# Linear attention: the row sums of the queries' exponentials taken by VectorE from a transpose, in place of matmuls with a block matrix

## Chip, cores and metric

The kernel runs on one core of one Trainium2 chip. The metric is the device time of one execution in microseconds (us), of which lower is better. Engines: PE is TensorE, PEld its weight loads, DVE is VectorE, ACT is ScalarE, POOL is GpSimd, SP is SyncE, which issues the DMAs.

## The reference, cut to what matters

The program runs four blocks on x, of shape 8 x 256 x 1024 in float32: a linear attention, a feed-forward with 4-bit weights, an autocorrelation attention and a second feed-forward. Only the first block is touched:

```python
def _L0_xattn_ref(q, k, v):
    B, C, N = q.shape            # 8, 256, 1024
    dh = C // H                  # H = 8, so 32 rows to a head
    qh = q.transpose(0, 2, 1).reshape(B, N, H, dh)
    kh = k.transpose(0, 2, 1).reshape(B, N, H, dh)
    vh = v.transpose(0, 2, 1).reshape(B, N, H, dh)
    qh = jax.nn.softmax(qh, axis=3)
    kh = jax.nn.softmax(kh, axis=1)
    kvs = jnp.einsum('bnhd,bnhe->bhde', kh, vh)
    out = jnp.einsum('bnhd,bhde->bnhe', qh, kvs)
    return out.transpose(0, 2, 3, 1).reshape(B, C, N)
...
x = x + jnp.tanh(g_xattn[0]) * _L0_xattn_ref(_layernorm(x, axis=-1), ctx_4096, ctx_4096)
```

The queries' softmax runs over the 32 rows of a head, for each of the 1024 columns. Its denominators are sums over 32 of the 128 rows of a tile.

## The kernel before

`phase_linear_attention` works on 16 tiles of 128 rows x 1024 columns in float32, one tile to a step i, with buffers of two. Each engine runs its own written-out order; `step(i, h)` is that order for one step, and semaphores join the engines. Three stages overlap: step i works on the attention of tile i, finishes the output of tile i-1, and normalises and transposes tile i-2 for the feed-forward that follows.

For one tile the work passes through the engines like this, with the lines of the profile:

- ACT computes `eq`, the exponential of the normalised queries (L417), and `ek`, that of the keys (L421, with its row sums).
- PE transposes `ek` into `psE` (L479). Then it takes the head sums of `eq` (L485): eight matmuls, in each of which a 128x128 piece of `eq` is multiplied with `blk`, a block-diagonal matrix of ones in blocks of 32. The result in `psB` has a column of `eq` on each partition and holds every sum 32 times.
- DVE takes the reciprocal of every 32nd element of it into `rS`, 128x32 (L553).
- ACT spreads each reciprocal over 32 places into `rSx` (L450), PE transposes that back into `psB` (L503), and ACT copies it to SBUF (L456, which releases `turned_done`).
- POOL multiplies `eq` by it (L399). That releases the output matmuls of PE (L492), which run one step later in program order, and DVE adds their result to `X` (L556).
- PE also multiplies the transposed keys with the context (L498), and DVE normalises and masks the product (L568). DVE computes the mean and variance of tiles ahead and behind (L521, L524); POOL turns them into an inverse root (L390, L392) and DVE into an offset (L529).
- ACT normalises the finished tile for the next phase (L463), PE transposes it (L509), and ACT and DVE store it in two half-precision parts (L426, L543). ACT also starts the next phase's weights (L438).

Two orders matter here. On POOL, the multiplication L399 of tile i stands ahead of the inverse root of tile i+2. On DVE, the offset of tile i+2 (L529) stands at the end of a step, and the next step begins with L543, L550 and L553:

```python
def step(i, h):                                   # POOL
    if exists(i - 1):
        rsqrt(i - 1, 1 - h, mv2, ve2, rstd2, mv2_done, rstd2_done)
    if exists(i):
        pool.wait_ge(turned_done, i + 1)
        pool.tensor_tensor(eq[h][:], rSx[:], eq[h][:], ALU.mult).then_inc(eqn_done, 1)
    if exists(i + 2):
        rsqrt(i + 2, h, mv, ve, rstd, mv_done, rstd_done)
```

ACT waits for `rS_done` ahead of L450, and the exponentials of tile i+1 (L417, L421) stand behind L450 in its order. In the last steps `ffn_scales` adds small instructions to every engine.

Of the kernel before, what the change touches and what calls it, by code (L numbers as in the profile page):

```python
# [24 lines left out]
AX = mybir.AxisListType  # L25

P = 128
B, L, D = 8, 256, 1024
# [10 lines left out]
ROWS0 = L // HEADS0  # L39
# [247 lines left out]
def phase_linear_attention(nc, io, res):  # L287
# [9 lines left out]
    with ExitStack() as ctx:  # L297
# [51 lines left out]
        with nc.Block() as block:  # L349
# [61 lines left out]
            @block.scalar  # L411
            def _(act):
                def exponentials(i, h):
                    act.wait_ge(nmr_done, i + 1)
                    after(act, out_mm, i - 1)
                    settle(act)
                    act.activation(eq[h][:], X[:, i, :], ACT.Exp, scale=rstd[h][:], bias=nmr[h][:]).then_inc(eq_done, 1)  # L417
                    after(act, ekT_mm, i - 1)
                    after(act, rks_done, i - 1)
                    act.wait_ge(ncm_done, i + 1)  # L420
                    act.activation(ek[h][:], c_in[h][:], ACT.Exp, bias=ncm[h][:], accum_out=ksum[h][:]).then_inc(ek_done, 1)  # L421

                def turned_high(i):
                    act.wait_ge(xT_mm, i + 1)
                    settle(act)
                    act.activation(halves_of(i, 0), turned_bank(), ACT.Copy, scale=LN_SCALE).then_inc(hi_done, 1)  # L426

                def first_kinks(i):

                    turn, k = divmod(i - 1, len(kinks))  # L430
                    if 0 <= turn < 2:
                        scale, bias, alpha = kinks[k]
                        act.wait_ge(res["first_in"], 16 * (AHEAD // 2) * (turn + 1))
                        if k:
                            act.wait_ge(res["kink_done"], AHEAD // 2 * (i - 1))
                        for u in range(AHEAD // 2 * turn, AHEAD // 2 * (turn + 1)):
                            block_u = res["first"][:, u, :]
                            act.activation(block_u, block_u if k else block_u.bitcast(I32), ACT.Prelu, bias=bias, scale=scale, alpha=alpha).then_inc(res["kink_done"], 1)  # L438

                def step(i, h):  # L440
                    if exists(i):
                        after(act, kv_mm, i - 1)
                        act.wait_ge(ekT_mm, i + 1)
                        act.activation(ekT[h][:], psE[:], ACT.Copy).then_inc(ekT_done, 1)
                    first_kinks(i)
                    if exists(i):
                        after(act, eqn_done, i)
                        act.wait_ge(rS_done, i + 1)

                        act.activation(rSx[:].rearrange("p (n r) -> p n r", r=ROWS0), rS[h][:].unsqueeze(2).to_broadcast([P, D // ROWS0, ROWS0]),  # L450
                                       ACT.Copy).then_inc(rSx_done, 1)
                    if exists(i + 1):
                        exponentials(i + 1, 1 - h)
                    if exists(i):
                        act.wait_ge(rS_mm, i + 1)
                        act.activation(rSx[:], psB[:], ACT.Copy).then_inc(turned_done, 1)  # L456
                    if i == TILES:
                        turned_high(i - 2)
                    if exists(i - 1):
                        after(act, xT_mm, i - 2)  # L460
                        act.wait_ge(nmr2_done, i)
                        settle(act)
                        act.activation(xn[1 - h][:], X[:, i - 1, :], ACT.Identity, scale=rstd2[1 - h][:], bias=nmr2[1 - h][:]).then_inc(xn_done, 1)  # L463
                    if exists(i - 2) and i != TILES:
                        turned_high(i - 2)

                exponentials(0, 0)
                act.wait_ge(const_in, 64)
                act.activation(tg[:], gates[:], ACT.Tanh).then_inc(tanh_done, 1)
                run(act, step, scales_act)  # L470

            @block.tensor
            def _(pe):
                def step(i, h):
                    if exists(i):
                        after(pe, kvm_done, i)
                        pe.wait_ge(ek_done, i + 1)
                        for k in range(KD):
                            mm = pe.transpose(psE[:, k * P:(k + 1) * P], ek[h][:, k * P:(k + 1) * P], ident[:])  # L479
                        mm.then_inc(ekT_mm, 1)  # L480

                        after(pe, turned_done, i)
                        pe.wait_ge(eq_done, i + 1)
                        for k in range(KD):
                            mm = pe.matmul(psB[:, k * P:(k + 1) * P], eq[h][:, k * P:(k + 1) * P], blk[:], start=True, stop=True)  # L485
                        mm.then_inc(sums_mm, 1)
                    if exists(i - 1):
                        pe.wait_ge(eqn_done, i)
                        pe.wait_ge(kvm_done, i)
                        after(pe, x_done, i - 1)  # L490
                        for n in range(2):
                            mm = pe.matmul(psO[:, n * BANK:(n + 1) * BANK], kvm[1 - h][:], eq[1 - h][:, n * BANK:(n + 1) * BANK], start=True, stop=True)  # L492
                        mm.then_inc(out_mm, 1)
                    if exists(i):
                        pe.wait_ge(ekT_done, i + 1)
                        pe.wait_ge(cT_in[h], (i // 2) * 16 + 16 if isinstance(i, int) else (i - h) * 8 + 16)
                        for k in range(KD):
                            mm = pe.matmul(psE[:, 0:P], ekT[h][:, k * P:(k + 1) * P], cT[h][:, k * P:(k + 1) * P], start=(k == 0), stop=(k == KD - 1))  # L498
                        mm.then_inc(kv_mm, 1)

                        pe.wait_ge(rSx_done, i + 1)
                        for k in range(KD):
                            mm = pe.transpose(psB[:, k * P:(k + 1) * P], rSx[:, k * P:(k + 1) * P], ident[:])  # L503
                        mm.then_inc(rS_mm, 1)
                    if exists(i - 2):
                        pe.wait_ge(xn_done, i - 1)
                        after(pe, lo_done, i - 2)
                        for k in range(KD):
                            mm = pe.transpose(psX[:, k * P:(k + 1) * P], xn[h][:, k * P:(k + 1) * P], ident[:])  # L509
                        mm.then_inc(xT_mm, 1)  # L510

                pe.wait_ge(const_in, 64)
                run(pe, step, scales_pe)

            @block.vector
            def _(dve):
# [28 lines left out]
                def step(i, h):  # L545
                    if exists(i - 3) and i != TILES + 1:
                        turned_low(i - 3)
                    if exists(i):
                        dve.wait_ge(ek_done, i + 1)
                        dve.reciprocal(rks[h][:], ksum[h][:]).then_inc(rks_done, 1)  # L550
                        dve.wait_ge(sums_mm, i + 1)

                        dve.reciprocal(rS[h][:], psB[:, 0:D:ROWS0]).then_inc(rS_done, 1)  # L553
                    if exists(i - 1):
                        dve.wait_ge(out_mm, i)
                        dve.scalar_tensor_tensor(X[:, i - 1, :], psO[:], tg[:, 0:1], X[:, i - 1, :], ALU.mult, ALU.add).then_inc(x_done, 1)  # L556
                        if i == TILES:
                            scales_dve(dve, "top")
                        dve.wait_ge(x_done, i)
                        stats(i - 1, 1 - h, st2, mv2, mv2_done)  # L560
                        if i == TILES:
                            scales_dve(dve, "every")
                            turned_low(i - 2)
                    if exists(i):
                        dve.wait_ge(rks_done, i + 1)
                        dve.wait_ge(kv_mm, i + 1)

                        dve.scalar_tensor_tensor(kvm[h][:], psE[:, 0:P], rks[h][:], blk[:], ALU.mult, ALU.mult).then_inc(kvm_done, 1)  # L568
                    if exists(i - 1):
                        offset(i - 1, 1 - h, mv2, rstd2, nmr2, rstd2_done, nmr2_done)  # L570
                    if exists(i + 2):
                        prepare(i + 2, h)
# [2209 lines left out]
```

## Time and profile before

| what | us |
|---|---|
| median of 3 runs (1981.24 to 1986.48) | 1981.4 |
| the profiled execution | 1980.49 |
| its span, first to last instruction | 1978.7 |
| busy in the span: PE | 1917.6 |
| DVE | 1268.1 |
| ACT | 1248.2 |
| POOL | 821.5 |

The span of the profiled execution covers all but 1.8 us of its own time. "Busy" is the time in which an engine has an instruction in it. Matmuls are pipelined and overlap, so that a busy PE can still be short of work. The linear attention occupies about the first 175 us of the span.

### The profile page before, as it was taken

What the parts mean: (1) busy time and instruction counts of PE and PEld (TensorE: products, weight loads), DVE (VectorE), ACT (ScalarE), POOL (GpSimd) and SP (SyncE); (2) the same over time, 40 slices, a digit from 0 to 9 for tenths busy, and PEclk for the clock granted to TensorE, in tenths of its full rate; (3) what the DMA queues carried; (4) which work ended last, traced back from release to release, by engine and by line L of the source; (5) the groups of instructions that cost most, each with busy time, mean ns of one, the idle gap of its engine ahead of it and who ended that gap; (6) DMA issues with size and microseconds to landing.
All of it is one profiled execution on the core that took longest, in us unless ns stands there. A gap on an engine that the chain in (4) does not pass through costs nothing. (4 is left out here: it accounts for less than half of the span.)

```text
span 1978.7 us, 26460 instructions
## 1 busy us (share of the span) xinstructions
PE 1917.6 (97%) x9188; PEld 965.9 (49%) x9188; DVE 1268.1 (64%) x2184; ACT 1248.2 (63%) x1988; POOL 821.5 (42%) x746
## 2 busy tenths in 40 slices
PE   6996999999999999999999999999998899999998
PEld 5774444444444444444444444444444455555544
DVE  5776666573645747365463745546389988888872
ACT  6886888667876777676777767766534434344431
POOL 2433644532222232232322323222268767767742
PEclk9998999999999999999999999999999999999999
DMA  5641633348667383754737466462551110111001
GB/s 208 215 169 54 249 98 100 99 171 283 197 212 235 114 279 109 242 201 165 266 100 265 150 218 205 155 245 83 205 165 33 33 53 27 44 53 38 27 22 43
DMA packets 89972, 288.33 MB, mean 146 GB/s; under 512 B 11760, under 2 KB 16496, under 8 KB 72944
## 3 DMA queue, kind: packets, MB, share of 16 engines
q1 hardware_dynamic: 89840, 286.64, 43.2%
q8 instruction: 74, 1.21, 0.3%
q14 instruction: 58, 0.48, 0.1%
HBM read 259.33 MB, written 27.26 MB: 145 GB/s over the span
## 5 line engine op out<-in xcount | busy, mean ns | idle before, releaser
L1034 ACT ACTIVATE first<-first 128x512 f32<-128x512 f32 (+1 forms) x1024 | 635.8, 626 | 26.3 <-DVE wt L1443 1.8
L1268 POOL TENSOR_TENSOR gu<-wt,gu 128x512 f16<-128x512 f32 x86 | 102.3, 1190 | 388.4 <-ACT gu L1055 388.4
L1443 DVE SCALAR_TENSOR_TENSOR wt<-first,w_scale,absm 128x512 f32<-128x512 f32 x132 | 102.9, 780 | 236.9 <-ACT first L1034 236.4
L1790 PE MATMUL a_psQ<-z,gu 128*128 128x512 f16 x840 | 187.2, 379 | 0.0
L2393 PE MATMUL a_psL<-z,l_x 128*128 128x512 f16 x768 | 170.7, 379 | 0.9 <-DVE l_x L2495 0.8
L1790 PE MATMUL a_psC<-z,gu 128*128 128x512 f16 x660 | 151.3, 379 | 0.0
L1790 PE MATMUL a_psC<-z 128*128 128x512 f16 x612 | 140.4, 379 | 0.0
L1446 DVE SCALAR_TENSOR_TENSOR wt<-a_psE,lora_gain,wt 128x512 f32<-128x512 f32 x132 | 99.1, 751 | 52.3 <-PE a_psE L1748 26.8
L1790 PEld LDWEIGHTS a_psQ<-z,gu 128*128 128x128 f16 x840 | 82.2, 98 | 99.1
L1268 POOL TENSOR_TENSOR dn_lo<-wt,dn_hi 128x512 f16<-128x512 f32 x42 | 49.0, 1167 | 192.3 <-ACT dn_hi L1055 192.3
L1280 POOL TENSOR_TENSOR hid_lo<-z,hid_hi 128x512 f16<-128x512 f32 x68 | 80.9, 1204 | 109.6 <-ACT hid_hi L1096 109.5
L1055 ACT ACTIVATE gu<-wt 128x512 f16<-128x512 f32 x86 | 53.4, 621 | 103.5 <-DVE wt L1446 79.6
L2393 PEld LDWEIGHTS a_psL<-z,l_x 128*128 128x128 f16 x768 | 75.0, 98 | 88.9 <-issue 1.2
L1505 DVE SCALAR_TENSOR_TENSOR X<-a_psL,ffn_gain,X 128x512 f32<-128x512 f32 x132 | 95.3, 745 | 24.5 <-PE a_psL L1847 24.4
L1268 POOL TENSOR_TENSOR z<-wt,z 128x512 f16<-128x512 f32 x51 | 59.8, 1187 | 103.1 <-ACT z L1055 103.1
L1847 PE MATMUL a_psL<-dn_hi,hid_hi 128*128 128x512 f16 x268 | 101.6, 379 | 0.2 <-DVE X L1505 0.2
L1847 PE MATMUL a_psL<-dn_hi,hid_lo 128*128 128x512 f16 x268 | 101.5, 379 | 0.0
L1505 DVE SCALAR_TENSOR_TENSOR X<-a_psQ,ffn_gain,X 128x512 f32<-128x512 f32 x106 | 77.7, 746 | 36.6 <-PE a_psQ L1847 36.6
L1790 PEld LDWEIGHTS a_psC<-z,gu 128*128 128x128 f16 x660 | 63.8, 98 | 74.2
L1505 DVE SCALAR_TENSOR_TENSOR X<-a_psC,ffn_gain,X 128x512 f32<-128x512 f32 x108 | 78.8, 746 | 32.6 <-PE a_psC L1847 32.6
L1847 PE MATMUL a_psL<-dn_lo,hid_hi 128*128 128x512 f16 x254 | 96.2, 379 | 0.0
L1790 PEld LDWEIGHTS a_psC<-z 128*128 128x128 f16 x612 | 59.4, 98 | 70.5
(418 smaller groups left out, 4167.2 us busy)
## 6 DMA issues: line engine op xcount, KB each, us to landing
z<-x_parts SPq DMA_DIRECT2D x126, 1024.0 KB, 6.0
first<-in_codes SPq DMA_DIRECT2D x132, 256.0 KB, 3.0
absm<-in_absmax SPq DMA_DIRECT2D x264, 128.0 KB, 3.4
X<-in_x SPq DMA_DIRECT2D x16, 512.0 KB, 4.4
c_in<-in_ctx SPq DMA_DIRECT2D x16, 512.0 KB, 5.3
cT<-in_ctxT SPq DMA_DIRECT2D x16, 512.0 KB, 3.5
o_sp<-in_w SPq DMA_DIRECT2D x16, 512.0 KB, 4.8
z<-in_ctx SPq DMA_DIRECT2D x8, 1024.0 KB, 7.3
```

The costliest lines, as they stand in the source:

```text
L1034: act.activation(level[w % 2][:], codes[w % RING] if k == 0 else level[w % 2][:], ACT.Prelu, bias=bias, scale=scale, alpha=alpha).then_inc ...
L1055: act.activation(dest(c, name, 0), wt[slot(name)], ACT.Copy).then_inc(whi_done, 1)
L1268: pool.tensor_tensor(low, source, high, ALU.subtract).then_inc(wlo_done, 1)
L1280: pool.tensor_tensor(low, buf, high, ALU.subtract).then_inc(hidlo_done, 1)
L1443: dve.scalar_tensor_tensor(wt[at], source[:], w_scale[:, m:m + 1], absm[w % RING][:], ALU.mult, ALU.mult).then_inc(scaled, 1)
L1446: dve.scalar_tensor_tensor(wt[at], ps_lora[w % 2], lora_gain[:, m:m + 1], wt[at], ALU.mult, ALU.add).then_inc(wt_done, 1)
L1505: dve.scalar_tensor_tensor(dst, ps_ring[down_bank(j, n)], ffn_gain[:], dst, ALU.mult, ALU.add).then_inc(acc_done, 1)
L1790: mm = pe.matmul(out, w[:, k * P:(k + 1) * P], xx[:, k], start=first and q == 0, stop=q == 3 * KD // 2 - 1, skip_group_check=True)
L1847: mm = pe.matmul(ps_ring[down_bank(j, n)], hh[c][:, i * P:(i + 1) * P], w[c][:, hf * BANK:(hf + 1) * BANK], start=(q == 0), stop=(q == len ...
L2393: mm = pe.matmul(sum_bank(d, half), a[:, ks], w[:, k, half * CB:(half + 1) * CB], start=(q == 0), stop=(q == 3 * KD - 1))
```

## The change

The matmul with `blk` becomes a transpose with the identity, so that `psB` holds the exponentials themselves, with a column of `eq` on each partition. DVE then sums each group of 32 elements itself, and takes the reciprocal in place as a second instruction behind a wait on its own semaphore. ACT's wait counts two increments to a tile.

```diff
@@ ACT
                         after(act, eqn_done, i)
-                        act.wait_ge(rS_done, i + 1)
+                        act.wait_ge(rS_done, 2 * i + 2)
@@ PE
                         for k in range(KD):
-                            mm = pe.matmul(psB[:, k * P:(k + 1) * P], eq[h][:, k * P:(k + 1) * P], blk[:], start=True, stop=True)
+                            mm = pe.transpose(psB[:, k * P:(k + 1) * P], eq[h][:, k * P:(k + 1) * P], ident[:])
                         mm.then_inc(sums_mm, 1)
@@ DVE
                         dve.wait_ge(sums_mm, i + 1)
 
-                        dve.reciprocal(rS[h][:], psB[:, 0:D:ROWS0]).then_inc(rS_done, 1)
+                        dve.reduce_sum(rS[h][:], psB[:].rearrange("p (n r) -> p n r", r=ROWS0), AX.X).then_inc(rS_done, 1)
+                        dve.wait_ge(rS_done, 2 * i + 1)
+                        dve.reciprocal(rS[h][:], rS[h][:]).then_inc(rS_done, 1)
```

The order of DVE's instructions around the edit, in a step of the middle of the phase. `made` is the buffer that holds `rS` and the other small tensors; `z` takes the half-precision parts. Before:

```order
L529 SCALAR_TENSOR_TENSOR made<-made 128x1 [waits rstd_done]
L539 TENSOR_SCALAR made<-made 128x1 [waits cmax_done]
L543 SCALAR_TENSOR_TENSOR z<-psX,z 128x2x512 [waits hi_done]
L550 RECIPROCAL made<-made 128x1 [waits ek_done]
L553 RECIPROCAL made<-psB 128x32 [waits sums_mm]
L556 SCALAR_TENSOR_TENSOR X<-psO,tg,X 128x1024 [waits out_mm]
```

And with the change:

```order
L529 SCALAR_TENSOR_TENSOR made<-made 128x1 [waits rstd_done]
L539 TENSOR_SCALAR made<-made 128x1 [waits cmax_done]
L543 SCALAR_TENSOR_TENSOR z<-psX,z 128x2x512 [waits hi_done]
L550 RECIPROCAL made<-made 128x1 [waits ek_done]
L553 TENSOR_REDUCE made<-psB 128x32 [waits sums_mm]
L555 RECIPROCAL made<-made 128x32 [waits rS_done]
L558 SCALAR_TENSOR_TENSOR X<-psO,tg,X 128x1024 [waits out_mm]
```

One instruction has come in, in the same place of the order; the lines behind it are numbered higher by two. On the other engines no instruction has come, gone or moved.

## Rows read from the trace of the kernel before

**Rows 1.** Busy time of each engine in one step (count of instructions), then granted clock
```profile
105.16:114.48 9.32, 8.54 (x63) 7.06 (x61) 7.23 (x16) 8.26 (x11) 3.91 (x5) 1.00 0.51 171
```

**Rows 2.** Timeline, one step: start us, us, engine, line, idle before
```profile
104.11 1.00 ACT L456 ACTIVATE wt<-psB 128x1024 f32<-128x1024 f32 x1
...
105.19 2.36 POOL L399 TENSOR_TENSOR eq<-wt,eq 128x1024 f32<-128x1024 f32 x1 [0.45 <-ACT wt L456]
105.25 1.97 PE L485 MATMUL psB<-blk,eq 128*128 128x128 f32 x16
...
107.61 1.98 PE L492 MATMUL psO<-eq,made 128*128 128x512 f32 x4 [0.39 <-POOL eq L399]
107.82 0.57 POOL L392 TENSOR_TENSOR made<-made,mhalf 128x1 f32<-128x1 f32 x1
...
108.43 0.16 DVE L529 SCALAR_TENSOR_TENSOR made<-made 128x1 f32<-128x1 f32 x1 [0.81 <-POOL made L392]
...
108.57 1.22 DVE L543 SCALAR_TENSOR_TENSOR z<-psX,z 128x1024 f16<-128x1024 f32 x1
...
109.77 0.34 DVE L553 RECIPROCAL made<-psB 128x32 f32<-128x32 f32 x1
...
110.20 1.06 ACT L450 ACTIVATE wt<-made 128x1024 f32<-128x1024 f32 x1 [1.06 <-DVE made L553]
...
111.31 1.09 PE L503 MATMUL psB<-ident,wt 128*128 128x128 f32 x8
...
112.30 1.13 ACT L421 ACTIVATE ek<-c_in,made 128x1024 f32<-128x1024 f32 x1
...
113.43 1.00 ACT L456 ACTIVATE wt<-psB 128x1024 f32<-128x1024 f32 x1
```

**Rows 3.** Waits from 40 to 150 us: total us, times, longest
```profile
ACT wt L450 <- DVE made L553: 12.6, 12, 1.1
```

**Rows 4.** Groups of DVE instructions: busy us, mean ns of one, idle before
```profile
L536 DVE TENSOR_REDUCE made<-c_in 128x1 f32<-128x1024 f32 x16 | 18.7, 1166 | 0.0
L553 DVE RECIPROCAL made<-psB 128x32 f32<-128x32 f32 x16 | 5.4, 340 | 3.9 <-PE psB L485 3.9
L2557 DVE RECIPROCAL rws<-wsum 128x4 f32<-128x4 f32 x15 | 2.7, 178 | 0.5
L224 DVE TENSOR_REDUCE made<-p_b 128x66 f32<-128x1056 f32 x1 | 1.2, 1241 | 0.0
```

**Rows 5.** Timeline, the sums of the first tile on PE
```profile
14.11 2.58 PE L485 MATMUL psB<-blk,eq 128*128 128x128 f32 x16
```

**Rows 6.** Timeline, the second and third steps
```profile
25.86 1.28 DVE L556 SCALAR_TENSOR_TENSOR X<-psO,tg,X 128x1024 f32<-128x1024 f32 x1 [0.65 <-PE psO L492]
...
28.53 1.01 ACT L456 ACTIVATE wt<-psB 128x1024 f32<-128x1024 f32 x1
...
29.43 0.57 POOL L392 TENSOR_TENSOR made<-made,mhalf 128x1 f32<-128x1 f32 x1
29.96 2.35 POOL L399 TENSOR_TENSOR eq<-wt,eq 128x1024 f32<-128x1024 f32 x1
30.03 2.30 DVE L529 SCALAR_TENSOR_TENSOR made<-made 128x1 f32<-128x1 f32 x1 [0.84 <-POOL made L392]
...
34.98 0.16 DVE L529 SCALAR_TENSOR_TENSOR made<-made 128x1 f32<-128x1 f32 x1
```

**Rows 7.** Timeline, the last tile's reciprocal and its reader
```profile
155.05 0.34 DVE L553 RECIPROCAL made<-psB 128x32 f32<-128x32 f32 x1
...
158.01 1.04 ACT L450 ACTIVATE wt<-made 128x1024 f32<-128x1024 f32 x1
```

**Rows 8.** Two stretches in the columns of rows 1, and PE's transposes in the second
```profile
162.00:164.00 2.00, 0.26 (x1) 0.26 (x2) 1.97 (x6) 2.00 (x4) 1.69 (x1) 1.00 0.00 0
171.00:173.00 2.00, 1.30 (x6) 1.30 (x7) 0.59 (x6) 0.64 (x1) 1.34 (x1) 0.50 0.00 0
...
171.70 1.97 PE L509 MATMUL psX<-ident,absm 128*128 128x128 f32 x8 [3.77 <-ACT absm L463]
```

## The prediction

> **What bounds the kernel now.** First the busy time of one step. PE has an instruction in it for 8.54 of 9.32 us, ACT for 8.26, DVE for 7.23, POOL for 3.91 [rows 1]. By shares alone PE looks like the bound, and the change halves one of its jobs. So the second view is the timeline of that step, read for what each instruction waited for [rows 2]. PE waits for POOL ahead of its output matmuls (0.39 us), and its head sums L485 are done at 105.25 + 1.97 = 107.22, while their reader L553 starts at 109.77. PE is 2.55 us early: nobody waits for these matmuls.
>
> Following the waits instead gives a closed loop over three engines [rows 2]. ACT's copy L456 (104.11) releases POOL's multiplication L399 (105.19, 2.36 us). Behind it POOL computes the inverse root (L392, done 108.39), which releases DVE's offset L529 (108.43, after 0.81 idle). Then DVE does L543 (1.22 us) and the reciprocal L553 (109.77 to 110.11), and that releases ACT's L450 (110.20, after 1.06 idle). ACT goes on without a pause through L417 and L421 (112.30) to the next L456 at 113.43. From 104.11 to 113.43 is 9.32 us, one step, with no slack anywhere. The sum of waits says the same: ACT waited for L553 in 12 of 12 steps, 1.05 us each [rows 3]. DVE's idle 0.81 us lies ahead of the place of the edit, in the loop too, and cannot absorb work that comes behind it.
>
> **The change part by part.**
>
> The PE side. Eight matmuls of 128x128 took 16 passes and 1.97 us; eight transposes of the same shape (L503) take 8 passes and 1.09 us [rows 2]. That frees 0.88 us a step, and costs or gains nothing from the second tile on, since the sums are 2.55 us early. Were that cover gone, the step would gain at most 0.88 us. Only the first tile's reader waited for PE (3.9 us, the only such wait in the group [rows 4]). There the 16 passes took 2.58 us [rows 5]; eight transposes at half clock take 1.97 us [rows 8]. Gain there: 0.61 us.
>
> The DVE side, which is in the loop. The reduction of 128x1024 to 128x32 out of PSUM is not in the trace. Bounds: 1166 ns for 1024 elements to 1, and 1241 ns for 1056 to 66 [rows 4]. I take the second less 32 elements at the slope between large reductions, about 1 ns an element: 1.21 us. It has many outputs, like the new one, and PSUM sources show no penalty (L543 reads 1024 elements from it in 1.22 us). The reciprocal of 128x32 now reads SBUF; the one before took 340 ns, one of 4 elements 178 ns [rows 4]. The extra elements cost time whatever the source, so I take 0.33, bounds 0.18 and 0.36. It waits for the reduction. For that wait I take 0.04, as L529 starts 0.04 us after the end of the POOL instruction that releases it; ACT's L450 starts 0.09 after its releaser, the upper bound [rows 2]. Together 1.21 + 0.04 + 0.33 - 0.34 = **1.24 us a step**, bounds 1.05 (1.166 + 0.04 + 0.18 - 0.34) and 1.35 (1.241 + 0.09 + 0.36 - 0.34). Behind the new pair in DVE's order are the X update L556, the statistics and the mask. All of them, and ACT's L450 with the exponentials behind it, move together, so their distances stay and the new step is 9.32 + 1.24 = 10.56 us. DVE is then busy 8.47 of it and is not the bound by itself.
>
> What of 16 steps counts:
> - Tile 0: 1.24 - 0.61 = +0.63 us.
> - Tile 1: +1.24, running sum 1.87.
> - Tile 2 is special. Before, POOL's L399 started at 29.96, just ahead of DVE's L529 at 30.03, and L529 then took 2.30 us in place of 0.16 [rows 6]. Both run beside each other there, and I read the 2.30 us as DVE held up by POOL; in the steady step L529 (108.43) meets no running L399 and takes 0.16. With the change the two separate. L399 hangs on L456, which moves by 1.87 to 30.40, so L399 starts 1.08 later (as in rows 2), at 31.48. The X update L556 had idled 0.65 us for the output matmul [rows 6]. It now follows the reciprocal directly and moves by only 1.13, and with it the end of L392, from 30.00 to 31.13. L529 starts at 31.16, is done at 31.32, and misses POOL by 0.16 us. From there POOL leads: in the steady step the next L529 starts 3.24 us after L399 (108.43 - 105.19), here at 34.72, where it stood at 34.98 [rows 6]. So DVE comes 0.27 us earlier to the sums of tile 2, and with the tile's own 1.24 the running sum is +0.97.
> - Tiles 3 to 14: 12 x 1.24 = 14.88.
> - Tile 15: L553 ends at 155.39 and ACT takes it up only at 158.01 [rows 7], 2.6 us later. Zero. Were that cover gone it would be 1.24.
>
> Sum 0.97 + 14.88 = **15.9 us**. The later phases begin that much later and are otherwise untouched. Against the profiled execution's 1980.5 us this is 1996.4. The median of the runs is 0.9 us higher, so 1997.3 beside 1981.4, or 0.8% slower.
>
> **TensorE's clock.** In the steady step the granted clock is 1.00 (2.4 GHz) [rows 1], and it stayed there in a stretch with PE busy 0.26 of 2 us [rows 8]. Before the change the longest run in which PE does only transposes goes from L503 (111.31) to the next L485 (105.25 + 9.32 = 114.57), 3.3 us; after it goes on to L492 (116.93 + 1.24 of stretch, counted from an L503 that is 1.24 later), 5.6 us, with about 4.3 us of transposes in it. I expect the clock to hold, as PE keeps some two thirds of the time filled. The Trainium skill, "TensorE: Matmul & The Clock Gate", Part 4, says that transposes do not count as activity of PE in the same way as matmuls. By that rule the clock could fall in each such run, which is the third rival; the trace can neither show nor refute it, since it has no run of transposes that long.
>
> **The rivals.**
> - *PE was the bound after all* (faster). PE would give 16 x 0.88 = 14.1 us, and DVE would absorb its part in the 2.1 us that it idles a step: 1967.3. It decides where L485 ends after DVE is free. For: 8.54 of 9.32 busy. Against: the 2.55 us above and every wait of the loop. Chance 0.03.
> - *The reduction is hidden* (no change). DVE idles 2.1 us a step, more than the 1.24 added. It would need slack behind L553, and ACT waits there in each step. 1981 to 1985; chance 0.04.
> - *The clock falls.* The granted clock goes to 0.50 (1.2 GHz) where PE runs short of work, as by 171 us [rows 8]. That makes eight transposes 1.97 us [rows 8]. Four groups are 7.9 us; the two groups of true matmuls, 1.98 each, stay or double: 11.8 to 15.8 us of PE work against a step of 10.56. PE becomes the bound, by 1.2 to 5.2 us in some 13 steps: 2013 to 2065, in the middle 2039. Chance 0.06.
> - *POOL and DVE collide in the steady step.* In the timeline L399 starts at 105.19, and the offset that was released before it had to be through by then; nothing in my count moves the two against each other. If it went, each step would lose up to 2.1 us as at 30.03: 2022. In the weaker form only the collision at tile 2 stays. Then the gain of 2 us there is not had: 1999.3. Chances 0.03 and 0.15.
> - *Main case:* loop lengthened, collision gone: 0.69. The bounds per step enter 15 times (tiles 0 to 14): 1981.4 + 15.9 - 15 x 0.19 = 1994.4, and + 15 x 0.11 = 1999.0.
>
> **Range and chances.** The main case and the weaker collision hold 0.84 together. With the bounds they reach from 1994.4 to 1999.0 + 2.0 = 2001.0; for terms that I have overlooked at the two ends of the phase I widen to 1992 to 2003. What is outside is the other rivals. The measurement tells about 0.3%, or 6 us, from no change. Slower than that are all but the first two rivals: 0.69 + 0.15 + 0.03 + 0.06 = 0.93. Within it 0.04, faster 0.03.
>
> **What would show it right or wrong.** Right: a step of about 10.56 us in the middle of the phase; a TENSOR_REDUCE of about 1.21 us 16 times and a reciprocal of about 0.33; ACT waiting some 2.3 us ahead of L450 in place of 1.06; PE's L485 in 8 passes of about 1.06 us together; waiting of PE for POOL up by about 0.9 a step plus the stretch; clock 1.00; L529 at 0.16 us in all steps; all later phases alike but shifted. Wrong: a step near 9.3, or a reduction far from 1.2 us, or a granted clock under 1.00 between 20 and 170 us.

## The result, and the profile after

| | before | after |
|---|---|---|
| median, us (4 runs each) | 1983.05 | 2000.09 |
| lowest to highest | 1981.24 to 1986.48 | 1998.63 to 2002.55 |
| profiled execution | 1980.49 | 1999.01 |
| its span | 1978.7 | 1996.9 |

The ratio of after to before is 1.0082, with a 95% interval of 1.0069 to 1.0095. The change makes the kernel slower by 0.8%: 16 us by the ratio, 17.0 by the two medians of the table. It was forecast at 1997.3 with a range of 1992 to 2003, beside 1981.4 for the kernel before.

First the same step of the loop as in [rows 2], from the timeline of the changed kernel (start us, us, engine, line, idle before):

```profile
109.02 0.15 DVE L550 RECIPROCAL made<-made 128x1 f32<-128x1 f32 x1
109.09 1.21 DVE L553 TENSOR_REDUCE made<-psB 128x32 f32<-128x1024 f32 x1
110.33 0.35 DVE L555 RECIPROCAL made<-made 128x32 f32<-128x32 f32 x1
...
110.79 1.06 ACT L450 ACTIVATE wt<-made 128x1024 f32<-128x1024 f32 x1 [2.30 <-DVE made L555]
...
111.90 1.09 PE L503 MATMUL psB<-ident,wt 128*128 128x128 f32 x8 [1.20 <-ACT wt L450]
...
114.02 1.00 ACT L456 ACTIVATE wt<-psB 128x1024 f32<-128x1024 f32 x1
...
114.68 0.16 DVE L529 SCALAR_TENSOR_TENSOR made<-made 128x1 f32<-128x1 f32 x1 [0.84 <-POOL made L392]
...
115.09 2.36 POOL L399 TENSOR_TENSOR eq<-wt,eq 128x1024 f32<-128x1024 f32 x1 [0.45 <-ACT wt L456]
115.16 1.04 PE L485 MATMUL psB<-ident,eq 128*128 128x128 f32 x8
...
117.51 1.98 PE L492 MATMUL psO<-eq,made 128*128 128x512 f32 x4 [1.32 <-POOL eq L399]
...
121.36 1.05 ACT L450 ACTIVATE wt<-made 128x1024 f32<-128x1024 f32 x1 [2.31 <-DVE made L555]
```

L450 starts at 110.79 and again at 121.36: the step is 10.57 us, where it was 9.32. The sum takes 1.21 us and the reciprocal 0.35. ACT's wait for them has grown from 1.06 to 2.30 us. PE's L485 is indeed shorter, 1.04 us in place of 1.97, and all of that has turned into waiting: PE now stands 1.32 us ahead of L492 (0.39 before) and 1.20 us ahead of L503, where it had not waited.

The sum of waits between 40 and 150 us, against [rows 3] (us in total, times, longest):

```profile
ACT wt L450 <- DVE made L555: 23.1, 10, 2.3
...
PE psO L492 <- POOL eq L399: 14.5, 11, 1.3
...
PE psB L503 <- ACT wt L450: 11.9, 10, 1.2
```

ACT now waits 2.31 us in each of the 10 steps that fit into the same stretch, where it was 1.05 in 12. The groups that answer to [rows 4] (busy us, mean ns, idle before):

```profile
L553 DVE TENSOR_REDUCE made<-psB 128x32 f32<-128x1024 f32 x16 | 19.3, 1206 | 3.3 <-PE psB L485 3.3
L555 DVE RECIPROCAL made<-made 128x32 f32<-128x32 f32 x16 | 5.7, 353 | 0.6
```

The start of L450 for chosen tiles shows where the time was lost. "End of the phase" is the start of POOL's first small instruction of the next phase.

| start, us | before | after | difference |
|---|---|---|---|
| first transpose L479 | 12.34 | 12.54 | 0.20 |
| L450 of tile 0 | 17.11 | 17.90 | 0.79 |
| tile 1 | 25.30 | 27.34 | 2.04 |
| tile 2 | 35.63 | 36.78 | 1.15 |
| tile 14 | 147.49 | 163.65 | 16.16 |
| tile 15 | 158.01 | 174.17 | 16.16 |
| end of the phase | 176.43 | 194.28 | 17.85 |
| end of the span | 1978.7 | 1996.9 | 18.2 |

Between tile 15 and the end of the phase 1.7 us were added that belong to TensorE's clock, whose granted value is 0.71 from 180 to 190 us. The timeline of PE there:

```profile
179.91 2.93 PE L492 MATMUL psO<-eq,made 128*128 128x512 f32 x4 [2.67 <-POOL eq L399]
182.63 1.82 PE L509 MATMUL psX<-ident,wt 128*128 128x128 f32 x8
```

In the profile of before the same two took 1.98 and 1.04 us, behind the same idle 2.67 us. Whether this has to do with the change is a question for the experiments.

### The profile page after: what moved, and what is told of

Read it like the earlier page. It is cut to its first block and busy times, and to the rows that moved or that the text cites. A ratio compares the mean times of both kernels' runs of the same rounds, so it can differ in the third digit from the quotient of the medians.

```text
span 1996.9 us, 26220 instructions
## 1 busy us (share of the span) xinstructions
PE 1906.3 (95%) x9060; PEld 952.2 (48%) x9060; DVE 1287.2 (64%) x2200; ACT 1247.8 (62%) x1988; POOL 821.3 (41%) x746
```

## Experiments

Theory: the step is set by the loop ACT L456, POOL L399, L390 and L392, DVE L529, L543 and sum or reciprocal, ACT L450, L417, L421, L456. PE is early in it. Rivals: PE is the bound, or the clock of PE carries the loss. A second theory had come with tile 2: POOL's L399 holds up DVE's offset L529 when it is running first.

### Each half of the change alone

The first kernel, e1, keeps only the transposes, and leaves the sums out:

```diff
-mm = pe.matmul(psB[...], eq[h][...], blk[:], start=True, stop=True)
+mm = pe.transpose(psB[...], eq[h][...], ident[:])
 dve.reciprocal(rS[h][:], psB[:, 0:D:ROWS0]).then_inc(rS_done, 1)
```

> Only the PE half of the change: transposes in place of the block matmuls, and DVE still takes the reciprocal of every 32nd element as before, so the sums over 32 rows are left out. Theory (a loop over ACT, POOL and DVE sets the step, PE is early): the step stays at 9.32 us, only the first tile gains up to 0.6 us, and the whole time stays within 3 us of the kernel before; L529 still takes about 2.3 us once. Rival (PE is the bound): 16 x 0.88 = 14 us faster, step near 8.4. Rival (fewer passes let the clock fall at the end of the phase): the step stays, but L492 of the last tile takes about 2.9 us in place of 1.98 and the phase ends 1 to 2 us later than in the kernel before.

Measured: 1983.46 us beside 1984.48 for the kernel before, ratio 0.9997 (0.9988 to 1.0007). From its timeline:

```profile
104.34 1.04 PE L485 MATMUL psB<-ident,eq 128*128 128x128 f32 x8
...
106.70 1.98 PE L492 MATMUL psO<-eq,made 128*128 128x512 f32 x4 [1.33 <-POOL eq L399]
...
108.86 0.34 DVE L553 RECIPROCAL made<-psB 128x32 f32<-128x32 f32 x1
109.30 1.06 ACT L450 ACTIVATE wt<-made 128x1024 f32<-128x1024 f32 x1 [1.06 <-DVE made L553]
```

L450 goes from 99.97 to 109.30: 9.33 us a step, with ACT waiting 1.06 us as before. The 15 us of PE work that were removed are worth nothing beyond the first tile. There L450 started 0.96 us earlier (16.15 for 17.11), more than the 0.61 forecast, since the eight transposes took 1.63 us: the clock rose in their midst. PE was not the bound. (That the clock rose is read from their duration, which lies between 1.04 and 1.97 us; the column of the granted clock shows 1.00 there from the start.) The last tile's L492 took 1.98 us, so half the passes alone did not bring the clock down there.

The second, e2, keeps the block matmuls and has only the DVE half. Each value that DVE sums already is the sum, so its results are 32 times too large and the attention's part of the output 32 times too small.

```diff
 mm = pe.matmul(psB[...], eq[h][...], blk[:], start=True, stop=True)
-dve.reciprocal(rS[h][:], psB[:, 0:D:ROWS0]).then_inc(rS_done, 1)
+dve.reduce_sum(rS[h][:], psB[:].rearrange("p (n r) -> p n r", r=ROWS0), AX.X).then_inc(rS_done, 1)
+dve.wait_ge(rS_done, 2 * i + 1)
+dve.reciprocal(rS[h][:], rS[h][:]).then_inc(rS_done, 1)
```

> Only the DVE half: the block matmuls stay (16 passes), and DVE sums each group of 32 and takes the reciprocal behind a wait, as in the changed kernel; each sum is then 32 times too large, so the attention's output is divided by 32. Theory: step 10.57 us as in the changed kernel, +1.25 on each, 16 to 18 us slower than before. If the last 1.7 us of the changed kernel's loss (clock at half for the last output matmuls) come from the halved PE work, they are gone here: 16.2 us, and L492 of the last tile takes 1.98 us. If they come from where the longer step puts the end of the phase, they stay or vary. Rival (PE is the bound): more than the changed kernel by 14 us, above 2010.

Measured: 1999.55 us, ratio 1.0081 (1.0061 to 1.0100), and the step is 10.59 us. DVE's half alone gives the changed kernel's whole loss. The two halves add up: -0.0003 and +0.0081 against +0.0082. In its second step, from 22 to 26 us, the granted clock was 0.61 and 0.54, and L485 took 3.21 us; from L450 of tile 0 to that of tile 1 it was 9.70 us, where the changed kernel has 9.44.

### Twice the sum

Kernel e8 is the changed kernel with the reduction done a second time:

```diff
-dve.reduce_sum(rS[h][:], psB[:].rearrange(...), AX.X).then_inc(rS_done, 1)
-dve.wait_ge(rS_done, 2 * i + 1)
+for n in range(2):
+    dve.reduce_sum(rS[h][:], psB[:].rearrange(...), AX.X).then_inc(rS_done, 1)
+    dve.wait_ge(rS_done, 3 * i + 1 + n)
```

> The changed kernel with the reduction done twice, each behind a wait. Theory (reduction plus wait are in the loop with no cover at all): each step grows by 1.206 + 0.03 = 1.24 us again, to 11.81; tiles 0 to 14 count, 18.5 us more than the changed kernel: 2016 to 2021. Rival (part of the first reduction was covered, or DVE gets full and the cost is larger): a growth per step that is not 1.24.

Measured: 2022.63 us, ratio 1.0193 (1.0178 to 1.0209). The step is 11.85 us, 1.27 more than the changed kernel's 10.57 and near the 1.24 forecast; nothing of it was covered. The total is 22.5 us above the changed kernel's and not 18.5, and above the forecast range. L450 of tile 15 was 19.1 us later; another 2.5 us came between it and the end of the phase. The collision of [rows 6] stands there again, behind the last tile's statistics:

```profile
197.13 2.34 POOL L399 TENSOR_TENSOR eq<-wt,eq 128x1024 f32<-128x1024 f32 x1
197.19 2.29 DVE L529 SCALAR_TENSOR_TENSOR made<-made 128x1 f32<-128x1 f32 x1 [0.84 <-POOL made L392]
```

In the changed kernel the offset in that place took 0.16 us (176.79). Here the clock also moved in the steady steps, which it had done in none of the kernels above. The first fence is one stretch in the columns of [rows 1], the granted clock being 0.91; the second is PE's timeline:

```profile
100.00:120.00 20.00, 14.60 (x88) 12.06 (x89) 15.75 (x30) 16.43 (x20) 7.85 (x10) 0.91 0.74 228
```
```profile
65.46 1.09 PE L503 MATMUL psB<-ident,wt 128*128 128x128 f32 x8 [2.45 <-ACT wt L450]
...
77.30 1.48 PE L503 MATMUL psB<-ident,wt 128*128 128x128 f32 x8 [2.45 <-ACT wt L450]
78.58 1.91 PE L509 MATMUL psX<-ident,absm 128*128 128x128 f32 x8
80.28 1.52 PE L479 MATMUL psE<-ident,ek 128*128 128x128 f32 x8
```

In some steps the transposes behind the 2.45 us wait ran at half clock (1.91 us for eight), in others not. The loop has enough room to hide it.

### The sums taken earlier in DVE's order

If the reciprocal is on the loop only through its place behind the offset L529, then another place should cut the loop. PE has the sums of tile i+1 ready before DVE needs them. Kernel e3 is the kernel before with this:

```diff
 def prepare(i, h):
     ...
     dve.reduce_max(cm[h][:], c_in[h][:], AX.X).then_inc(cmax_done, 1)
+    if i >= 2:
+        sums(i - 1, 1 - h)     # waits for sums_mm, then the reciprocal of before
     offset(i, h, mv, rstd, nmr, rstd_done, nmr_done)
```

In the old place the reciprocal stays for tile 0 alone, and that of the last tile is taken at the end of the step ahead of it, where no `prepare` is called.

> The kernel before with one reordering: the reciprocal of tile i+1's sums is taken at the end of step i, behind the reduction of the keys and ahead of the offset that waits for POOL, instead of in step i+1 behind that offset and the half-precision store. Theory: the loop through POOL, L529, L543 and the reciprocal is cut; L450 then starts when ACT is free (some 1.05 us earlier), and the next bound is ACT's own 8.3 us or PE's loop L456, L399, L492, L498, L503 of about 8.4. Step 8.4 to 8.6, 14 tiles: 10 to 13 us faster than before, 1969 to 1972. Rival (the wait for the reciprocal is not what sets the step): within 2 us of before.

Measured: 1988.14 us, ratio 1.0019 (1.0010 to 1.0029): a miss, slower and not faster. The steps explain it. L450 started at 82.89, 93.91, 102.32, 113.34 and 121.74, so they are 11.02 and 8.41 us in turn. The first theory was right about the loop: the short step is the one that was forecast. But the other step holds this:

```profile
98.06 0.16 DVE L529 SCALAR_TENSOR_TENSOR made<-made 128x1 f32<-128x1 f32 x1 [0.84 <-POOL made L392]
...
98.21 2.36 POOL L399 TENSOR_TENSOR eq<-wt,eq 128x1024 f32<-128x1024 f32 x1 [0.19 <-ACT wt L456]
...
106.88 2.35 POOL L399 TENSOR_TENSOR eq<-wt,eq 128x1024 f32<-128x1024 f32 x1
106.94 2.30 DVE L529 SCALAR_TENSOR_TENSOR made<-made 128x1 f32<-128x1 f32 x1 [0.84 <-POOL made L392]
```

At 98 us L529 comes first and takes 0.16. At 107 L399 starts 0.06 us ahead of it, and it takes 2.30. It is the collision of [rows 6], now in every second step. Kernel e4 is the changed kernel with its sum and reciprocal in that same place, and it met the collision in nearly every step:

> The changed kernel with the same reordering: the sum and the reciprocal of tile i+1 are taken ahead of the offset that waits for POOL. Theory: the idle 0.8 us of DVE ahead of that offset takes up part of the 1.6 us of sum and reciprocal, the rest delays the offset, which is no longer in ACT's way. DVE becomes the bound with 8.48 us busy and one remaining wait of about 0.85: step 9.2 to 9.5, so 1980 to 1984, some 16 us faster than the changed kernel, but slower than the block version with the same order. Rival: the added work costs the same wherever it stands, 1998 to 2000.

Measured: 2016.94 us, ratio 1.0164 (1.0142 to 1.0185), steps of 11.80 us, L529 at 2.3 us in 13 of them. That is a miss too, with the same cause.

### Removing the collision in two ways

The first way makes POOL wait with L399 until the offset is through. Kernel e6 is e3 with it, e7 is e4 with it:

```diff
 pool.wait_ge(turned_done, i + 1)
+after(pool, nmr2_done, i)
 pool.tensor_tensor(eq[h][:], rSx[:], eq[h][:], ALU.mult).then_inc(eqn_done, 1)
```

> e3_block_early with one wait more on POOL: L399 starts only when DVE's offset of the tile before (nmr2_done) is through. In e3 every second step had L529 at 2.30 us beside a POOL L399 that started 0.06 us ahead of it. Theory (POOL holds DVE's offset up, nothing else keeps e3 from its gain): L529 is 0.16 or less in all steps, each step is 8.5 to 8.9 us, 12 to 14 steps gain 0.4 to 0.8 us each: 5 to 11 us faster than the kernel before. Rival (another loop sets e3's step): no faster than before.

Measured: 1980.47 us, ratio 0.9982 (0.9969 to 0.9994). The collision is gone (32 offsets of 160 ns in the mean, 613 in e3), and each step is 9.05 us, slightly above the forecast 8.5 to 8.9. The gain is some 3 us, short of the 5 to 11 forecast. A new loop sets the step: POOL L399, L390 and L392, DVE's offset, its half-precision store, the X update and the statistics, POOL L390 and L392, DVE's other offset, and L399 again, 0.34 us of it being the added wait. PE's output matmuls are not in it: from 40 to 150 us the X update never waited for them.

> e4_transpose_early with the same wait on POOL. Theory: without the collisions the step is 9.3 to 9.6 us, DVE bound (8.48 busy and 0.85 of waiting for POOL): 1981 to 1988, 12 to 18 us faster than the changed kernel, still slower than e6. Rival: stays above 1995.

Measured for e7: 1988.75 us, ratio 1.0028 (1.0018 to 1.0037), steps of 9.71 us, a little longer than expected. Without the collisions the sums cost far less in the early place. They still make the kernel slower than before, and 8.3 us (0.4%) slower than the same order with block matmuls.

The second way changes the instruction and adds no wait; e9 is e3 with it, and e10 is e4 with it. The offset has two small tensors in SBUF as operands; a tensor_scalar takes the inverse root as a scalar for each partition.

```diff
-dve.scalar_tensor_tensor(nm_[h][:], mv_[h][:, 0:1], -1.0, rs_[h][:], ALU.mult, ALU.mult)
+dve.tensor_scalar(nm_[h][:], mv_[h][:, 0:1], rs_[h][:], -1.0, ALU.mult, ALU.mult)
```

> e3_block_early without the wait of e6; instead DVE's offsets (L529) are written as a tensor_scalar, with the inverse root as a per-partition scalar, in place of a scalar_tensor_tensor with two tensors in SBUF. Theory A (the stall comes from an instruction with two SBUF tensors meeting POOL's L399, as other DVE instructions run beside L399 at their usual length): no offset longer than 0.2 us; the step is then set by the loop L399, L492, X update, statistics, L392 of 8.7 us (9.05 in e6 less the 0.34 that POOL waited): 10 us faster than before, 1971 to 1976. Theory B (any DVE instruction of this kind is held): every second offset still takes 2.3 us, and the time is e3's, 1985 to 1990.

Measured: **1976.03 us, ratio 0.9958 (0.9943 to 0.9973)**. The step is 8.72 us in nearly all tiles, as forecast; the time lies at the upper end of its range. POOL still starts first, and the offset no longer cares:

```profile
100.82 2.37 POOL L399 TENSOR_TENSOR eq<-wt,eq 128x1024 f32<-128x1024 f32 x1
100.89 0.21 DVE L529 TENSOR_SCALAR made<-made 128x1 f32<-128x1 f32 x1 [0.86 <-POOL made L392]
```

This is theory A in one row: 0.21 us where 2.30 stood. The price is 0.05 us an offset (211 ns in the mean for 160). It computes all that the kernel before does, and is the fastest of this study, ahead of the kernel before and the changed one.

> The changed kernel with the early sums and the offsets as tensor_scalar. Theory A: no collisions, DVE bound, step 9.3 to 9.7 (9.71 in e7, where DVE's wait of 0.34 behind POOL is part): 1983 to 1990, slower than e9 by more than 10 us. Theory B: as e4, 2012 to 2020.

Measured for e10: 1988.11 us, ratio 1.0023 (1.0013 to 1.0032), steps of 9.73 us. With the block matmuls in the same kernel it was 1976.03, so 12 us lie between the two ways to form the sums, even where both have the best place that was tried. DVE is then busy in 95.0 of the 110 us from 40 to 150 us.

### The collision at tile 2

Two kernels, each executed once, went to the part of the forecast that concerned tile 2. The first, e5, adds one reduction to the kernel before, in tile 1 alone:

```diff
+if i == 1:
+    dve.reduce_sum(rS[h][:], psB[:].rearrange(...), AX.X).then_inc(rS_done, 1)
+    dve.wait_ge(rS_done, 2)
 dve.reciprocal(rS[h][:], psB[:, 0:D:ROWS0]).then_inc(rS_done, 1)
```

> The kernel before with one reduction more, of tile 1 alone and its result not used: it stands where the changed kernel has its sum, behind the block matmuls. Theory: the delay of 1.24 us takes the offset L529 out of POOL's way: its one duration of 2.30 us becomes 0.16, and L450 of tile 2, at 35.63 in the kernel before, stands at about 34.8 (1.24 later for the reduction, some 2.1 earlier for the offset); from there on steps of 9.32. Rival (the 2.30 us has another cause than POOL's L399, or its loss was not on the path): L450 of tile 2 at 36.9, and L529 still 2.3 us once.

It took 1984.5 us. Half of it came true. L450 of tile 2 stands at 35.09, against 35.63 before, in an execution that was 0.34 us later at tile 0, so that 0.88 us were gained by adding work. The long offset did not vanish; it came one step later:

```profile
39.76 2.35 POOL L399 TENSOR_TENSOR eq<-wt,eq 128x1024 f32<-128x1024 f32 x1
39.83 2.30 DVE L529 SCALAR_TENSOR_TENSOR made<-made 128x1 f32<-128x1 f32 x1 [0.84 <-POOL made L392]
```

After a short step the statistics reach POOL late, L399 starts right behind L392, and DVE is second. The changed kernel has its sum in each step and stays clear of this. Nor did the gain last in e5: L450 of tile 3 comes 29.11 us after that of tile 0, where it was 27.84, so that by then the added reduction was paid in full.

The second, e11, is the kernel before with the new form of the offset and nothing else:

> The kernel before with nothing changed but the offsets as tensor_scalar. Theory A: the one long offset of 2.30 us at tile 2 is 0.2 or less, L450 of tile 2 stands about 2 us earlier (33.6 in place of 35.6), and the step stays at 9.32 from there, since the loop through POOL is untouched: 2 us faster. Theory B: the offset still takes 2.3 us and nothing moves.

No offset was longer than 0.21 us, and L450 of tile 2 came 16.79 us after that of tile 0, where it had been 18.52 (35.63 - 17.11). So 1.7 us were gained there. From tile 0 to tile 15 only 0.7 of it was left (140.17 us for 140.90): the next step was longer, and the steady ones were 9.37 us for 9.32, by as much as the new form of the offset is longer. The forecast of 2 us did not hold. The execution as a whole took 1988.1 us. It had begun its first transposes 1.2 us later (13.55), and its mean granted clock was 0.991. One execution cannot say whether this kernel is faster than before.

### What the clock does to a run

The runs of e1 give the kernel before 19 times, each with its mean granted clock. Where it was 0.996 they took 1980.69 to 1981.89 us; where it was 0.992 or 0.993, they took 1983.43 to 1987.88. The executions of the changed kernel do the same: 1998.63 and 1999.01 at 0.995, 2001.17 at 0.993 and 2002.55 at 0.991. From L450 of tile 15 to the end of the phase it took 18.3 to 18.5 us in the profiles of before, e1, e2, e6, e7 and e10, and 20.1 to 20.2 in those of after, e3, e5, e9 and e11. Transposes and block matmuls stand in both lists. (It took 22.7 in e8, with the collision above, and 22.5 in e4, where PE ran L498 in 3.78 us behind 3.55 us of waiting.) So the 1.7 us at the end of the phase in the profile of after are not an effect of halving PE's work alone. Each kernel was profiled once, so that it is not shown whether they go with the kernel or vary from one execution to the next, nor what decides it.

## Why the prediction was right

- **The bound.** The loop was named from the idle times in [rows 2], against PE's 8.54 of 9.32 busy us in [rows 1]. e1 shows it from one side (PE's work halved: nothing), e2 from the other (DVE's work alone: everything), and e3 and e9 by cutting it.
- **The price of the pair.** Forecast 1.21 + 0.04 + 0.33 - 0.34 = 1.24; measured 1.206 + 0.03 + 0.353 - 0.340 = 1.25. The step: 10.56 forecast, 10.57 measured. The reduction from PSUM cost what the wide SBUF reduction in [rows 4] gave less 32 elements. The reciprocal did cost the same from SBUF as from PSUM.
- **Tile 0.** Forecast +0.63; measured 0.79, of which 0.20 had been there before PE's first instruction, so 0.59. The eight transposes took 1.91 us, where 1.97 was forecast.
- **Tile 1.** Running sum forecast 1.87, measured 1.84 after the same 0.20.
- **Tile 2.** Forecast 0.97, measured 0.95. L529 stands at 31.23 with 0.16 us and L399 at 31.64; forecast were 31.16 and 31.48. That POOL is what holds the offset up was a reading of one row; e6 and e9 have shown it since.
- **Tiles 3 to 14, and 15.** Forecast 14.88, measured 15.01 (16.16 - 1.15); forecast 0 for tile 15, measured 0.
- **The sum.** 15.9 us forecast to the end of tile 15, 15.96 measured. The ratio gives about 16.3 us (0.0082 x 1983), with an interval of 14 to 19. The rest of the profiled difference of 18.5 is the late start (0.2), the clock at the end of the phase (1.7) and small remainders. The clock's share was missing in the working, which held the end of the phase to be the same in both kernels. The measured median, 2000.09, is 2.8 us above the forecast: 1.65 of it because the kernel before was itself 1983.05 in the comparison and not 1981.4. As a difference, the 17.0 us of the medians lie within the bounds of the main case (13.0 to 17.6); as a time, 2000.09 lies above its 1999.0, and it was the width added for other cases and overlooked terms that held it.
- **The clock rival.** The granted clock stayed at 1.00 from 20 to 180 us, although from L503 (111.90) to L492 (117.51) PE did transposes alone for 5.6 us. The page of the Trainium skill, "TensorE: Matmul & The Clock Gate", Part 4, would have let it fall there; this trace does not agree. Nor does the first tile of e1: up to 15.56 us PE had done nothing but sixteen transposes, and it was in their midst that they became faster. In e8, with PE idle for 2.45 us in each step besides, the clock did fall, to 0.91 from 100 to 120 us, and cost the step nearly nothing. No run has that idle time with the block matmuls, so that the part of the transposes in this fall is open; in e2 it fell in one early step with block matmuls.

## What to carry to other kernels

A share of busy time does not name the bound: an engine 92% busy here was 2.5 us early in each step, while 1.25 us on an engine 78% busy was paid in full, because the latter stood in a closed loop of waits. Before making an operation cheaper on one engine by moving part of it to another, follow the waits of one step until they close, and put the new work where the loop does not pass; the same reciprocal a few places earlier in DVE's order, with the offset written so that POOL cannot hold it up, made the step 0.6 us shorter. And where a loop has been cut, look at once for what the freed engines now run into.

## What the runs showed of the hardware

A DVE instruction on 128x1 elements took 2.30 us in place of 0.16 when it started 0.06 us behind POOL's tensor_tensor of 128x1024, and waited for the whole of it. With two tensors in SBUF it took 2.29 to 2.31 us each of the 24 times that it started behind a running L399 (before, e1, e3, e4, e5, e8); as a tensor_scalar with a per-partition scalar it was not held up (0.21 to 0.22 us, 29 times in e9, e10 and e11), nor were the statistics and reductions that ran beside L399 in all kernels. The Trainium skill states this in "SBUF — State Buffer", section "SBUF: two separate sides": VectorE and GpSimd share a pair of ports that is held for a whole instruction, and VectorE needs it with two SBUF inputs. Beside L399 the trace agrees, with 2.30 against 0.21 us, and shows that it applies to inputs of one element to a partition as well. Beside another instruction of POOL it does not agree. L201 is a tensor_tensor too, which raises one SBUF tensor to the power of another, and it lasts as long, but the same form of the offset, started 0.06 us behind it, took 0.16 us, here and in each of the ten profiles that have this form:

```profile
170.07 2.28 POOL L201 TENSOR_TENSOR absm<-absm,half 128x12 f32<-128x12 f32 x1
170.13 0.16 DVE L529 SCALAR_TENSOR_TENSOR made<-made 128x1 f32<-128x1 f32 x1
```

So POOL's instruction matters as well as DVE's. Whether it is the number of its elements (12 for 1024 in a partition) or the operation, no run tells apart.

A reduction of 1024 float32 elements to 32 sums in each partition took 1.21 us from PSUM, and a reciprocal of 32 elements 0.34 to 0.35 us from either memory.
